# A recommendation tower: the pairs inside two neighbouring chunks share one unit, and the last sums of the closing MLP begin earlier

## What is computed

```python
e = jnp.stack([tbl_0[ids[:, 0]], tbl_1[ids[:, 1]], ..., tbl_39[ids[:, 39]]], axis=1)
iidx, jidx = jnp.triu_indices(40, k=1)
z = jnp.einsum('bpd,pde,bpe->bp', e[:, iidx, :], bilinear_matrices, e[:, jidx, :])
h = jnp.concatenate([z, dense_ctx], axis=1)
h = jnp.maximum(h @ W_top1 + b_top1, 0.0)
h = jnp.maximum(h @ W_top2 + b_top2, 0.0)
y = h @ W_top3
```

## Time and profile before

| what | us |
|---|---|
| median of 3 runs (lowest, highest) | 1263.33 (1260.73, 1263.44) |
| the profiled execution | 1266.12 |
| its span, first to last instruction | 1264.3 |
| PE busy | 902.1 (71%) |
| DVE busy | 564.9 (45%) |
| GpSimd busy | 503.5 (40%) |
| ACT busy | 81.2 (6%) |
| mean granted TensorE clock | 0.796 of full |

### The profile page before, as it was taken

One profiled execution on the slowest core, in us unless ns is written; L12 is line 12 of the kernel. 1 busy time (PEld: TensorE's weight loads), 2 busy tenths in 40 slices (PEclk: granted clock), 3 DMA queues, 4 the chain that ended last, 5 costly groups with the idle time before them and its releaser, 6 DMA issues.

```text
span 1264.3 us, 18015 instructions
## 1 busy us (share of the span) xinstructions
PE 902.1 (71%) x7934; PEld 328.6 (26%) x7934; DVE 564.9 (45%) x623; ACT 81.2 (6%) x143; POOL 503.5 (40%) x535
## 2 busy tenths in 40 slices
PE   3111135668655867779867858669999899999999
PEld 1000012224332312223212312112222222224445
DVE  2000023225433523447645514437775467786662
ACT  2000020000000000000000000000000000001101
POOL 7777455652444265534324366443224420000000
PEclk7555556667777967769877967779999889999999
DMA  3003001120122200000100010000000000000000
GB/s 64 13 13 52 9 10 20 28 36 18 29 39 52 72 12 11 10 8 8 13 7 9 6 13 11 8 8 7 5 5 9 10 5 2 1 1 3 2 2 2
DMA packets 60880, 20.04 MB, mean 16 GB/s; under 512 B 46359, under 2 KB 59996, under 8 KB 60802
## 3 DMA queue, kind: packets, MB, share of 16 engines
q0 software_dynamic: 16896, 8.68, 5.0%
q1 hardware_dynamic: 43892, 10.18, 4.2%
q10 hardware_dynamic: 14, 0.03, 0.0%
HBM read 18.81 MB, written 0.04 MB: 15 GB/s over the span
## 4 chain that ended last, share of the span: by engine, by line
PE 61%; another core or an unknown queue 20%; issue 12%; DVE 3%; ACT 2%; DMA 1%; SPq 0%; ACTq 0%; DVEq 0%
PE U L653 24%; PE bank_z L670 17%; PE misc L700 10%; PE misc L609 6%; PE U L632 4%; DVE prod L562 3%; PE U L700 1%; DVE ones L541 0%; SPq L304 0%; DMA W<-_L_rec_bilinear_matrices 0%; PE bank_z L678 0%; ACT x_T L431 0%; ACT W L473 0%; DMA idx<-in_ids 0%
## 5 line engine op out<-in xcount | busy, mean ns | idle before, releaser
L389 POOL DMA_INDIRECT rows<-in_tbl,idx x528 | 502.7, 952 | 540.9 <-PE U L632 388.5
L562 DVE TENSOR_TENSOR prod<-U,x_T 128x1024 f32<-128x1024 f32 (+1 forms) x380 | 403.7, 1100 | 329.3 <-remote 174.8
L653 PE MATMUL U<-x_T,W 32*128 32x512 f32 (+1 forms) x1696 | 289.1, 600 | 107.8 <-issue 73.8
L670 PE MATMUL bank_z<-prod,select 128*32 128x512 f32 (+1 forms) x2100 | 267.9, 567 | 3.6 <-issue 3.5
L609 PE MATMUL misc<-ones,tabs 125*32 125x512 bf16 (+1 forms) x1050 | 124.7, 404 | 156.4 <-issue 153.9
L653 PEld LDWEIGHTS U<-x_T,W 32*128 32x128 f32 x1696 | 107.1, 203 | 257.8 <-issue 167.2
L562 DVE TENSOR_TENSOR prod<-U,x_look 128x1024 f32<-128x1024 f32 (+1 forms) x110 | 103.6, 968 | 137.0 <-PE U L653 80.1
L541 DVE TENSOR_SCALAR ones<-idx_wide,row_of 125x2048 bf16<-125x2048 f16 (+3 forms) x100 | 58.4, 604 | 208.1 <-remote 167.5
L700 PE MATMUL misc<-z,W 128*32 128x512 f32 (+1 forms) x952 | 138.3, 566 | 6.1 <-issue 4.3
L609 PEld LDWEIGHTS misc<-ones,tabs 125*32 125x32 bf16 x1050 | 47.4, 109 | 233.2 <-issue 216.4
L670 PEld LDWEIGHTS bank_z<-prod,select 128*32 128x32 f32 x2100 | 51.9, 114 | 186.1 <-issue 131.8
(11 more groups left out here) (48 smaller groups left out, 83.3 us busy)
## 6 DMA issues: line engine op xcount, KB each, us to landing
rows<-in_tbl,idx POOLq DMA_INDIRECT x528
idx_wide<-idx_rows SPq DMA_DIRECT2D x3, 500.0 KB
idx_wide<-idx_rows SPq DMA_DIRECT2D x3, 375.0 KB
W<-in_W_top SPq DMA_DIRECT2D x1, 512.0 KB
idx_wide<-idx_rows SPq DMA_DIRECT2D x2, 187.5 KB
W<-in_W_top SPq DMA_DIRECT2D x11, 32.0 KB
prod<-in_tbl SPq DMA_DIRECT2D x2, 156.2 KB
z<-in_tbl SPq DMA_DIRECT2D x2, 156.2 KB
```

What stands on the lines that cost most here:

```text
L389: nc.gpsimd.indirect_dma_start(out=rows[:, n % R_SLOTS, t, f, :], out_offset=None, in_=tables[field][:, :], in_offset=bass.IndirectOffsetO ...
L562: last = nc.vector.tensor_tensor(prod[:, (2 * g + h) % P_SLOTS, 0:R, m * N:(m + n) * N].rearrange("p r (m n) -> p r m n", m=n), U[:, at:at ...
L653: last = nc.tensor.matmul(U[:, at + r % 2, m * N:(m + 1) * N], W[r * DIM:(r + 1) * DIM, at_W:at_W + P], x_of(o, a)[r * DIM:(r + 1) * DIM, ...
L670: last = nc.tensor.matmul(bank_z[r * DIM:(r + 1) * DIM, 0:N], sel, prod[:, (2 * g + r // 2) % P_SLOTS, r % 2, m * N:(m + 1) * N], start=(k ...
```

## The change

Chunks 2k and 2k+1 share one unit for their inner pairs. The units (a, a) of odd a go away. A twin unit (a, a) of even a holds in columns 0 to 63 and 64 to 127 of its weights two kinds of pairs: those inside chunk a, and those inside chunk a+1, stored in the strips that were empty, fields in reverse order (`back_pairs`). Its right and left sides therefore mix both chunks. ACT copies them into a new tile `x_twin` (`copy_twin`, seven copies of 32 or 64 partitions for each of 25 twins, one buffer), once both chunks are there and the earlier twin's products are made. PE waits for `twin_copied` before the twin's cycle, and projects it with 8 matmuls of 32x64 in place of 4 of 32x128. DVE multiplies its first half in two pieces.

What follows from it: 50 units a block (last tile: two units and the dense inputs, still seven tiles), 200 cycles (25, 50, 50, 50, 25, all cycles of block 0 and 4 with two units). Chunk 9 has no units, so there is no W strip 0, and the first projection is that of chunk 8: PE's loop starts at g = -2 with turn (0, 8). The twin of chunk 0 comes first of its chunk, the others last. W_top1 comes in 93 pieces, W in 66 (39 before). The planner moves look-up (2, 1) from block 0 to block 1 and reorders the others. In SP's queue, W strips 5 to 9 go together ahead of wide load (1, 1), and wide loads (2, 1) and (4, 0) go behind W_top1 and the biases.

At the end the six first parts of result 0 go ahead of the last sum_up, then six parts of each other result, then the last tile's part of each of the four.

```diff
-UNITS = [(a, J) for a in CHUNK_OF_STEP for J in range(CHUNKS - 1, a - 1, -1)]
+def units_of(a):
+    twin = [(a, a)] if a % 2 == 0 else []
+    across = [(a, J) for J in range(CHUNKS - 1, a, -1)]
+    return across + twin if a else twin + across
+UNITS = [u for a in CHUNK_OF_STEP for u in units_of(a)]
 NU = len(UNITS)
-FIRST_UNIT = [UNITS.index((a, CHUNKS - 1)) for a in CHUNK_OF_STEP]
+FIRST_UNIT = {c: UNITS.index(units_of(a)[0]) for c, a in enumerate(CHUNK_OF_STEP) if units_of(a)}
...
-W_WIDTH = [P * (CHUNKS - a) for a in CHUNK_OF_STEP]
+W_WIDTH = [P * len(units_of(a)) for a in CHUNK_OF_STEP]
...
+def w_col(a, J):
+    return W_START[CHUNK_OF_STEP.index(a)] + P * (J - a - (a % 2))
+def back_pairs(a):
+    return [(CF - 1 - f, CF - 1 - g, pair(CF * (a + 1) + f, CF * (a + 1) + g))
+            for f in range(CF) for g in range(f + 1, CF)]
...
-place([("look", o, q) for o, q in ((1, 0), (0, 1), (2, 0), (1, 1), (3, 0), (2, 1))], 0, FIRST_CYCLE[1])
-place(mlp_jobs(0, (0, 1)) + [("look", 4, 0)] + mlp_jobs(0, (2, 3)) + [("look", 3, 1)] + mlp_jobs(0, (4, 5, 6))
-      + [("look", 4, 1)], FIRST_CYCLE[1], FIRST_CYCLE[2] - 1)
+place([("look", o, q) for o, q in ((1, 0), (0, 1), (2, 0), (1, 1), (3, 0))], 0, FIRST_CYCLE[1])
+place(mlp_jobs(0, (0, 1)) + [("look", 2, 1)] + mlp_jobs(0, (2, 3)) + [("look", 4, 0)] + mlp_jobs(0, (4, 5))
+      + [("look", 3, 1)] + mlp_jobs(0, (6,)) + [("look", 4, 1)], FIRST_CYCLE[1], FIRST_CYCLE[2] - 1)
...
+            TURN_AT[max(-2, CYCLE_OF[(_o, FIRST_UNIT[_c])] - (3 if _o else 2))].append((_o, _c))
...
+TWINS = [(o, a) for o in range(BLOCKS) for a in CHUNK_OF_STEP if a % 2 == 0]
+TWIN_CYCLE = [CYCLE_OF[(o, UNITS.index((a, a)))] for o, a in TWINS]
+TWIN_AT = {g: [] for g in range(-2, G)}
+for _n, (_o, _a) in enumerate(TWINS):
+    _turned = next(g for g in TURN_AT if (_o, CHUNK_OF_STEP.index(_a)) in TURN_AT[g])
+    TWIN_AT[max(_turned, TWIN_CYCLE[_n] - 3)].append(_n)
...
+                for r, q, p in back_pairs(a) if a % 2 == 0 else []:
+                    at = w_col(a, a) + q * DIM
+                    sp.dma_start(W[r * DIM:(r + 1) * DIM, at:at + DIM], bil[p]).then_inc(W_landed[c], 16)
...
-            load_W(5)
+            for c in range(5, CHUNKS):
+                load_W(c)
             load_wide(1, 1)
-            load_W(6)
             load_wide(3, 0)
-            load_W(7)
-            load_wide(2, 1)
-            load_W(8)
-            load_wide(4, 0)
-            load_W(9)
             for t, row, at, m in W1_LOADS:
                 sp.dma_start(W1[row:row + m, t, :], W_top1[at:at + m, :]).then_inc(mlp_loaded, 16)
...
+            load_wide(2, 1)
+            load_wide(4, 0)
...
+            def copy_twin(n):
+                (o, a), N = TWINS[n], ROWS[TWINS[n][0]]
+                c = CHUNK_OF_STEP.index(a)
+                if n:
+                    act.wait_ge(multiplied, 2 * (TWIN_CYCLE[n - 1] + 1))
+                for J in (a, a + 1):
+                    if GATHERED[CHUNK_OF_STEP.index(J)]:
+                        act.wait_ge(turn_kept, TURN[(o, CHUNK_OF_STEP.index(J))] + 1)
+                    if CHUNK_OF_STEP.index(J) in GROUP_OF_STEP:
+                        act.wait_ge(misc_kept, JOB[("look", o, GROUP_OF_STEP[CHUNK_OF_STEP.index(J)])] + 1)
+                for r in range(CF):
+                    nc.scalar.activation(x_twin[r * DIM:(r + 1) * DIM, 1, 0:N],
+                                         x_of(o, a + 1)[(CF - 1 - r) * DIM:(CF - r) * DIM, :], ACT.Copy)
+                for r in range(2):
+                    nc.scalar.activation(x_twin[r * DIM:(r + 1) * DIM, 0, 0:N],
+                                         x_of(o, a + 1)[(CF - 1 - r) * DIM:(CF - r) * DIM, :], ACT.Copy)
+                nc.scalar.activation(x_twin[2 * DIM:, 0, 0:N], x_of(o, a)[2 * DIM:, :], ACT.Copy
+                                     ).then_inc(twin_copied, 1)
...
+                    if UNITS[ks[m]][0] == Js[m]:
+                        if h == 0:
+                            nc.vector.tensor_tensor(to[:, 0, m * N:(m + 1) * N], U[:, at, m * N:(m + 1) * N],
+                                                    x_of(o, Js[m]), ALU.mult)
+                            last = nc.vector.tensor_tensor(to[:, 1, m * N:(m + 1) * N],
+                                                           U[:, at + 1, m * N:(m + 1) * N],
+                                                           x_twin[:, 0, 0:N], ALU.mult)
+                        else:
+                            last = nc.vector.tensor_tensor(to[:, :, m * N:(m + 1) * N],
+                                                           U[:, at:at + 2, m * N:(m + 1) * N],
+                                                           x_twin[:, :, 0:N], ALU.mult)
...
+                for k in ks:
+                    if UNITS[k] == (a, a):
+                        pe.wait_ge(twin_copied, TWINS.index((o, a)) + 1)
...
+                            for side in range(2):
+                                own = side == 0 and r == 0 or side == 1 and r < CF - 1
+                                x = x_of(o, a)[row, :] if own else x_twin[row, 1, 0:N]
+                                last = nc.tensor.matmul(U[side * P // 2:(side + 1) * P // 2, at + r % 2,
+                                                          m * N:(m + 1) * N],
+                                                        W[row, at_W + side * P // 2:at_W + (side + 1) * P // 2], x,
+                                                        start=True, stop=True, skip_group_check=True)
...
-            sum_up(G - 1)
             o, n = BLOCKS - 1, JOB[("mlp", BLOCKS - 1, 0)]
             pe.wait_ge(misc_kept, n)
-            for t in range(ZT):
-                for j in range(H1 // P):
-                    mlp(o, j, t, misc if j == 0 else U[:, j - 1, :])
+            for t in range(ZT - 1):
+                mlp(o, 0, t, misc)
+            sum_up(G - 1)
+            for j in range(1, H1 // P):
+                for t in range(ZT - 1):
+                    mlp(o, j, t, U[:, j - 1, :])
+            for j in range(H1 // P):
+                mlp(o, j, ZT - 1, misc if j == 0 else U[:, j - 1, :])
```

109 lines of the change are left out of this document (62 added, 47 removed).

## The result

Measured beside each other on one chip, 12 runs each: before 1267.27 us, after **1257.68 us** (1244.17 to 1272.93), ratio 0.9928, 95% interval 0.99 to 0.9955. Some 10 us are gained where 42 us were forecast, and the time lies above the range. The times of the two kernels overlap in part, but the interval of the ratio leaves 1 out, so the gain is small and real. The profiled execution of after has a span of 1253.1 us against 1264.3, 11.2 us less, so the two traces can be laid side by side.

What follows compares the result with a forecast made beforehand. PE's own work in the open stretches plus a fixed sum of stalls beside gather streams was taken as the bound. 60.8 us gained less 19 lost gave 41.8 net, from 1266.12 to 1224.3, by the median 1222 us; range 1198 to 1252.

Steps and rivals of the forecast that it cites:

- Fewer units, 512 rows: 33 us: Three 512-row blocks: 5 cycles fewer each, 29.4 us at full clock, 33 taken with a tenth on top, ends 29.4 and 36.
- Rival 5: DVE paces the 512-row cycles: 6 us gained a block, not 9.8; 1233 us; inside the forecast's 0.50, no separate chance.
- The 2 us for twins: Twin units in 512-row blocks: twice the projection instructions cost 0.15 us for each of 15 twins, 2 us lost.
- rival 1: Twin projections: two sides of one row strip run one after the other, price 18 us, 1240 us; chance 0.13.
- 256 rows: 15.8 gained, 8 lost: Two 256-row blocks: fewer cycles gain 15.8 us; alternating plain and twin forms costs 0.8 us for ten cycles, 8 us.
- W: 11 us: Block 0: PE's 11.1 us wait for the last strip of W goes, as strips 5 to 9 load earlier; 11 us gained.
- Copies: 3 us: ACT's seven copies a twin have two cycles (5 to 6 us) or more before PE needs them; 3 us lost, ends 0 and 50.
- Start: 3 us: First projection moves from 163.7 to 171.2, next stream stays at 166; 3 us lost, ends 0 and 8.
- Streams: 3 us: Gather streams move closer with fewer cycles between turns, block 4's short ones join up; 3 us lost, ends -5 and 20.
- rival 2: Streams eat half of the gain, open 8 us less well used: 1 us for each of 21 streams, 1243 us; chance 0.12.
- Closing MLP: 1 us: At the end, six parts go ahead of the last sum and the second layer starts without a gap; about 1 us gained.
- rival 3: Copies' hand-over falls into the gather stalls: 15 twins lose 4 us each, 60 us go, slower at 1282 us; chance 0.09.

Runs made afterwards that it cites:

- experiment 3: Changed kernel with x_twin filled once and ScalarE's copies left out: 766.25 us with gathers, 709.02 without; it also shows a timeline of the unedited changed kernel.
- an_nocopy: Changed kernel without its gathers and without ScalarE's twin copies, row buffers and x_twin filled once: 709.02 us, against 733.88 with the copies.

## Why the prediction was wrong, step by step

The direction was right, and the gains of the 512-row blocks and of W were there, both larger than forecast. The steps that failed are three terms of what is lost (the room for the copies, the start, the streams) and the price of a piece at 256 rows.

- **Fewer units, 512 rows: 33 us.** Without copies and gathers blocks 1 to 3 last 154.8, 149.8 and 151.2 us against 169.1, 162.5 and 162.3 with the strips in order: 38 us. The mechanism is right and its price low: 2.5 us for a cycle removed, nearer to DVE's two products (2.4) than to PE's 1.96. Rival 5 falls with it, as each block gains 11 to 14 us and not its 6. The 2 us for twins weren't spent: a twin's project at 512 rows takes 1.04 us (1103.09 to 1104.13 in experiment 3), against 1.07 of a plain one, so rival 1 falls too. Eight tiles of 32x64, two for each row strip, ran at once. The Trainium skill, TensorE: Matmul & The Clock Gate, Part 3: Packing small matmuls, says that a weight load overlaps matmuls in flight only when the row group differs; the trace doesn't agree, as all eight weight loads and matmuls start within 0.1 us and the first matmuls last 0.65.
- **256 rows: 15.8 gained, 8 lost.** Block 0 is 102.9 before and 103.6 us after (strips in order, no copies), block 4 92.7 and 92.5. Nothing is left of 7.8 us. The step that failed is the price of a piece: the sum took 0.45 us, half of what a double's sum takes; alone it takes 0.6, so a mixed double takes 2.44 and not 1.8 us, 4.43 at the low clock (block 0's first). Ten of them lose 10 x (2.44 - 1.09) = 13.5 us at full clock, about the 2 x 6.5 us that the fewer units give.
- **W: 11 us.** Measured 22 in the kernel before (with the look-up's move), 18 with most of it undone in the changed one. The forecast took the one wait that is put down to a DMA for the only one; two more, 5.26 and 8.40 us, stand in the same trace as "issue" in front of the same line.
- **Copies: 3 us.** Measured 24.9 with the start's share (an_nocopy has its first sum 3.5 us earlier). This is the step that cost most. The forecast gave every twin's copies two cycles of room, 5 to 6 us. For a twin in its chunk's first cycle (chunk 0's) it was one, 2.9 us: the turn stands at the end of the third cycle ahead and the project is one cycle early, while the eviction (0.59) and the copies (4.5) follow one another. The waits are 3.8 us in block 0 and 2.0, 2.5 and 2.5 in blocks 1 to 3; chunk 8's in block 4, also in a first cycle, waits 1.3. Chunk 8's in blocks 2 and 3 (2.6 and 1.8 us) and chunk 2's in block 1 (1.2) have a cycle more, and wait for another reason. In the trace without gathers their copies start 0.02 to 0.03 us behind ScalarE's eviction of z or of a look-up, which comes ahead of them in its order and itself waits for PE's last sum or part. The earlier twin's buffer is free long before.
- **Start: 3 us.** 17.8 on the chip of the forecast, 6.5 without gathers (first sum at 42.4 for 35.9; two other kernels with the same start have it at 40.8 and 41.1). The step that failed is "the next stream starts at 166 either way": it starts at 163.77. The 11 us between lie where the stream now starts 8 us ahead of PE's first project; that it is this overlap was argued from the trace, no run tried it on such a chip.
- **Streams: 3 us.** Blocks 1 to 3 win 1.3 us with gathers on the chip of the forecast and 11.4 without: 10 us go. This is rival 2 in kind, at half its price. "A stall lasts as long as GpSimd's stream" was read off; that it deepens with the stream was in the same trace and wasn't. Why these 10 us are lost isn't shown: in blocks 1, 2 and 3 the gathers cost the changed kernel 2.0, 4.8 and 3.3 us more than the one before.
- **Closing MLP: 1 us.** 0.8.

With these put in, 38 + 22 + 0.8 gained and 21.4 + 17.8 + 10 lost leaves 11.6 us net, with 18 for the strips 7.6, against 11.2 between the two spans. The terms come from several chips, and the 10 us are themselves a remainder, so that they meet so well is in part luck. What stands by itself is the pair of traces: without gathers the spans differ by 32.8 us, with gathers on the chip of the forecast by 11.2, and of the 21.6 between, 11.3 are in the start and 10.1 in blocks 1 to 3. Copies and start weigh about the same as all that the forecast called net; rival 3 (the hand-over of copies) named the right wait and overpriced it, by putting it into the stalls, while it mostly stands where there are none.

"The one number that would upset the whole" was named as the stall of a stream. It did so in part only: on the chips where it is absent the change brings no more than some 7 us, for another reason, GpSimd's 1.27 us a gather. What stays open: why some chips stall beside gathers and others don't, by what part of the chip, and whether the same chip always does.
